# Sorted rows: eight places in the first mixture part, and adding gathers for the second batch's results

## What is computed

```
x = x + 0.5 * moe(layernorm(x))
x = x + attention(layernorm(x))
x = x + 0.5 * moe(layernorm(x))

moe(x):    for each row pick the expert with the largest logit (8 experts), rw = sigmoid(top logit)
           g = (rw * x) @ w_gate[e].T ; u = (rw * x) @ w_up[e].T ; y = (u * silu(g)) @ w_down[e].T
attention: 8 heads of 64, keys and values from a latent of 64, softmax over 1024 keys, output projection
```

## Time and profile before

| | us |
|---|---|
| median of 3 runs | 1085.79 |
| the three runs | 1084.59, 1085.79, 1086.81 |
| profiled execution, own time | 1084.6 |
| its span, first to last instruction | 1082.8 |
| busy in the span: PE, DVE, POOL, ACT | 968.5, 704.0, 693.9, 483.8 |
| mean granted TensorE clock (1 is full) | 0.957 |

### The profile page before, as it was taken

One profiled execution on the slowest core, in us unless ns is written; L12 is line 12 of the kernel. 1 busy time (PEld: TensorE's weight loads), 2 busy tenths in 40 slices (PEclk: granted clock), 3 DMA queues, 4 the chain that ended last, 5 costly groups with the idle time before them and its releaser, 6 DMA issues.

```text
span 1082.8 us, 14843 instructions
## 1 busy us (share of the span) xinstructions
PE 968.5 (89%) x5084; PEld 519.7 (48%) x5084; DVE 704.0 (65%) x1197; ACT 483.8 (45%) x794; POOL 693.9 (64%) x400
## 2 busy tenths in 40 slices
PE   5799866999899899999999999999999998954995
PEld 3488633444344544444455444444544443443784
DVE  5765587477777746777765676776666676743563
ACT  4673322544444264444433444444244446331562
POOL 1345530899899366777854767786278788836554
PEclk9799966999999999999999999999999999967998
DMA  9365521212202100000010000001000300053321
GB/s 326 126 196 152 149 69 59 65 39 51 68 12 74 69 2 1 1 1 1 1 69 1 1 0 2 1 1 44 26 1 1 118 1 1 33 161 105 118 87 42
DMA packets 41688, 61.52 MB, mean 57 GB/s; under 512 B 7114, under 2 KB 35278, under 8 KB 40592
## 3 DMA queue, kind: packets, MB, share of 16 engines
q1 hardware_dynamic: 23616, 31.26, 8.6%
q0 software_dynamic: 9024, 18.69, 6.5%
q10 hardware_dynamic: 8976, 10.63, 2.8%
HBM read 28.28 MB, written 26.64 MB: 51 GB/s over the span
## 4 chain that ended last, share of the span: by engine, by line
PE 67%; DVE 17%; POOL 5%; ACT 3%; issue 3%; another core or an unknown queue 3%; DMA 1%; POOLq 0%; ACTq 0%; DVEq 0%
PE ps_o L1377 16%; PE ps L1364 11%; PE ps L1171 8%; DVE maxes L1177 7%; PE ps L835 7%; DVE rows_store L1749 5%; PE ps_x L1151 5%; POOL arena_b L1853 4%; PE ps L1530 3%; PE ps_x L1399 2%; PE ps_o L853 2%; PE ps L819 2%; PE ps_x L694 1%; PE ps_x L1243 1%
## 5 line engine op out<-in xcount | busy, mean ns | idle before, releaser
L1177 DVE TENSOR_REDUCE maxes<-ps 128x2 f32<-128x1024 f32 x256 | 310.8, 1217 | 195.4 <-PE ps L1171 194.8
L1853 POOL TENSOR_TENSOR arena_b<-arena_b 128x1024 f32<-128x1024 f32 x112 | 272.3, 2437 | 173.3 <-PE ps_o L1377 137.9
L1853 POOL TENSOR_TENSOR arena_b<-arena_b,hot_store 128x1024 f32<-128x1024 f32 x108 | 263.6, 2441 | 60.7 <-PE ps_o L1377 28.6
L1364 PE MATMUL ps<-q_split,keys_now 64*128 64x512 f32 x1536 | 205.5, 392 | 0.0
L1618 ACT ACTIVATE arena_b<-ps 128x1024 f32<-128x1024 f32 x144 | 143.2, 1022 | 101.5 <-PE ps L1364 101.4
L1364 PEld LDWEIGHTS ps<-q_split,keys_now 64*128 64x128 f32 x1536 | 145.2, 185 | 33.1 <-issue 4.1
L1377 PE MATMUL ps_o<-arena_b,latent_now 128*64 128x512 f32 x576 | 147.2, 613 | 1.3 <-ACT arena_b L1618 1.3
L1618 ACT ACTIVATE hot_store<-ps 128x1024 f32<-128x1024 f32 x112 | 111.9, 1021 | 57.4 <-PE ps L1364 57.4
L1377 PE MATMUL ps_o<-hot_store,latent_now 128*64 128x512 f32 x448 | 115.2, 610 | 2.6 <-ACT hot_store L1618 2.5
L1749 DVE RECIPROCAL rows_store<-rows_store 128x256 f32<-128x256 f32 (+1 forms) x72 | 112.6, 1565 | 6.5 <-ACT rows_store L1629 6.5
L835 PE MATMUL ps<-arena_a,arena_b 128*128 x368 | 100.9, 398 | 0.9 <-DVE arena_b L985 0.5
(11 more groups left out here) (294 smaller groups left out, 1155.6 us busy)
## 6 DMA issues: line engine op xcount, KB each, us to landing
sorted_y<-arena_b ACTq DMA_DIRECT2D x46, 128.0 KB
x_res<-sorted_x SPq DMA_DIRECT2D x32, 130.0 KB
x_res<-x_in SPq DMA_DIRECT2D x4, 1024.0 KB, 13.6
scaled_x<-rows_store SPq DMA_DIRECT2D x16, 256.0 KB, 2.1
keys_now<-keys_next SPq DMA_DIRECT2D x4, 1024.0 KB, 4.6
sorted_x<-blank SPq DMA_DIRECT2D x2, 1560.0 KB
sorted_x<-blank SPq DMA_DIRECT2D x2, 1430.0 KB
arena_a<-w_gu SPq DMA_DIRECT2D x1, 2048.0 KB, 15.6
```

The costliest lines, as they stand in the source:

```text
L1177: nc.vector.tensor_reduce(maxes[:, 2 * m:2 * m + 2], bank[:, :, :], AX_X, ALU.max) \
L1364: last = nc.tensor.matmul(ps_s[n % 2][:, a, :], keys_now[h, key, k], query[h, p, q], start=False, stop=(kt >= KT - STRIDE and query is q_h ...
L1853: nc.gpsimd.tensor_tensor(t, t, prob(k, kt).rearrange("p a n -> p (a n)"), ALU.add) \
```

## The change

The ring of sorted rows in f1 gets eight places instead of four; rows_back moves to the start of arena_b, over the raw weights, and leaves its room to the larger ring. POOL waits for the folds before the first gather back. DVE's adding of tiles 0 to 7 starts at step 39 instead of 43 and is spread over eleven steps (tiles at steps 40, 41, 43, 44, 45, 47, 48, 49). Tiles 8 to 15 are no longer gathered into rows_back and added by DVE: POOL joins them with eight adding gathers, which wait for nothing but their place in POOL's order. DVE waits for each four of them after one half of the keys, takes their statistics there, and makes the variance after the second half.

```diff
+IN_RING = {"f1": 8, "f2": RING}
-BACK_AT = SLOT_TILES - 3
+BACK_AT = SLOT_TILES - 7
...
-        rows_back = take(RING, D)
-        rows_in = take(RING, D)
+        rows_back = arena_b[:, 0:RING * D].rearrange("p (b n) -> p b n", b=RING)
+        rows_in = take(IN_RING["f1"], D)
...
-                h, k = t // AHEAD_TILES, t % RING
+                h, k = t // AHEAD_TILES, t % IN_RING["f1"]
...
-                if t >= RING:
-                    pool.wait_ge(sem("in_turned"), t - RING + 1)
+                if t >= IN_RING["f1"]:
+                    pool.wait_ge(sem("in_turned"), t - IN_RING["f1"] + 1)
...
+            pool.wait_ge(sem("folded"), 2 * PAIRS)
             for t in range(JOINED):
                 k = t % RING
-                if t >= RING:
+                if RING <= t < QT:
                     pool.wait_ge(sem("ffn_added"), t - RING + 1)
...
+                if t >= QT:
+                    pool.indirect_dma_start(x_tile(t), None, sorted_y[0][:, :],
+                                            bass.IndirectOffsetOnAxis(ap=slots[:, t:t + 1], axis=0),
+                                            compute_op=ALU.add).then_inc(sem(f"second{(t - QT) // GROUP}"), 16)
+                    continue
...
             for i in range(ROW_PAIRS):
                 dve_norm_rows(dve, 0, i)
-                gathered(QT + i)
-            for t in range(QT + ROW_PAIRS, JOINED):
-                gathered(t)
-            dve_variance(dve, "att", QT, JOINED)
             for j in range(2):
                 dve_keys(dve, 0, j, banks[4 + j])
+                dve.wait_ge(sem(f"second{j}"), 16 * GROUP)
+                for t in range(QT + j * GROUP, QT + (j + 1) * GROUP):
+                    tile_stats(t, "att")
+            dve_variance(dve, "att", QT, JOINED)
```

More of the change, by code:

```diff
@@ L219, in row_out @@
                 return sem(f"row_out{k}"), 16 * turn
-            name, uses = (("in{}_f1", len(range(k % RING, SLOT_TILES, RING))), ("gathered{}", JOINED // RING),
+            name, uses = (("in{}_f1", len(range(k % RING, SLOT_TILES, IN_RING["f1"]))), ("gathered{}", QT // RING),
                           ("joined{}", GROUP))[k // RING - 3]
@@ L811, in turn @@
                 if tag == "f1":
-                    pe.wait_ge(sem(f"in{k % RING}_f1"),
-                               16 * (t // RING + 1) if isinstance(t, int) else (t - k % RING) * 4 + 16)
+                    pe.wait_ge(sem(f"in{t % IN_RING['f1']}_f1"), 16 * (t // IN_RING["f1"] + 1))
                 else:
@@ L819, in turn @@
                     last = nc.tensor.transpose(banks[k % 2][:, c * P:(c + 1) * P],
-                                               source[:, k % RING, c * P:(c + 1) * P], ident[:, :])
+                                               source[:, t % IN_RING[tag], c * P:(c + 1) * P], ident[:, :])
                 last.then_inc(sem("in_turned"), 1)
```

## The result

The changed kernel takes 1091.2 us (median of 10 runs, 1088.96 to 1097.8) against 1084.95 for the kernel before beside it (1083.54 to 1088.24). The ratio is 1.0057, 95% interval 1.004 to 1.0074. The prediction said 1086.0, no measurable change, with a range that ends at 1089.2. It is slower, outside the range. The profiled execution took 1090.11 us with a span of 1088.3, 5.5 us more than before. One execution of experiment 10 (1204.59 us) and one of experiment 12 (5121.62 us) lay far above the others, and the ratios leave them out.

What follows compares the result with a forecast made beforehand. Bounds: PE in f1, then a chain hopping between engines, then DVE's maxima. Terms -1.5 - 0.9 + 2.6 = +0.2 us on the profiled 1084.6 gave 1084.8, median 1086.0; range 1082.6 to 1089.2.

Steps and rivals of the forecast that it cites:

- Eight places: Sorted gathers of f1: POOL four tiles further ahead, gathers back about 7 us earlier, DVE's adds earlier; gain 1.5 us.
- I take nothing: DVE's two early adds in f1 fit beside PE's matmuls and cost 0; 0.4 us if PE had no cover.
- the same five DMAs near 121 us: Last sorted gather and four gathers back, 1.26 us apart: same pace beside the same stores, only 7 us earlier.
- The last sorted gather at 113.4: End of f1: POOL issues its last sorted gather near 113.4 instead of 120.37 us, needing tile 37 turned, not 41.
- The stall near 126 us, taken as 0: Late f1, PE's steps 3.79 us apart, 2.1 lost: unchanged; bounds -2.1 if it goes, +2.1 if it comes twice.
- The rival that had it go: The stall near 126 us in f1 disappears, saving 2.1 us: 1083.9 us; chance 0.25.
- Slower, by a second stall: Rival: the eight adding gathers, at 134 to 149 us, bring another stall: 1088.6 or 1090 us; chance 0.16.
- nothing happened: Argument against a second stall: adding gathers are 1.86 us apart, and gathers 1.62 us apart had caused none.
- The square root, gain 1.5: Batch 0's variance after f1: square root right behind ACT's table load, at 138.4 instead of 139.95; gain 1.5 us.
- The turns, gain 0.9: Four PE turns before the latents, without DVE's adds between: last starts 3.3 us after the first, not 4.2; gain 0.9.
- The statistics behind the keys, loss 2.6: Eight statistics and variance moved into DVE's chain before the maxima: loss 0.35 + 2.25 us; bounds 0 and 3.7.
- Load on the DMA engines: Near 126 us: transfers from different engines share 16 DMA engines, so moving gathers among the same stores wins nothing.

Runs made afterwards that it cites:

- experiment 10: experiment 9 with four of the moved statistics ahead of the first keys, four with the variance between the key halves; 1083.81 us, ratio 1.0001.
- experiment 12: experiment 4 with two gaps of 1.4 us in the first 16 scatters of f2, behind the fifth and tenth; 1079.22 us, ratio 0.9962.
- experiment 1: The changed kernel with four places and DVE's adds from step 43 again, the rest of the change kept; 1085.47 us, ratio 1.002.
- experiment 2: The kernel before with eight places, rows back over raw weights, adds from step 39, second batch joined as before; 1087.19 us, ratio 1.0036.
- experiment 7: The changed kernel with a shorter POOL pause (128x256 memset) behind all 46 sorted gathers and the first four gathers back; 1085.01 us, ratio 0.9984.
- experiment 4: The kernel before with a POOL memset and wait behind its last sorted gather and first four gathers back; 1080.29 us, ratio 0.9969.
- experiment 3: The changed kernel with pauses behind its first twelve sorted gathers, eight at the half switch, the last, and four gathers back; 1088.13 us, ratio 1.0036.
- experiment 11: experiment 9 with the eight moved statistics reading 16 of 256 columns, part of the layer norm left out; 1080.19 us, ratio 0.997.
- experiment 9: experiment 1 with the pauses of experiment 4; 1082.96 us, ratio 0.9996 against the kernel before.
- experiment 6: The kernel before with 24 plain loads of 128 rows by SP into an unused buffer, POOL's gathers unchanged; 1084.76 us, ratio 0.9991.
- experiment 5: The kernel before with three more POOL gathers behind sorted gather 27 into unused places, still four ring places; 1091.13 us, ratio 1.0049.
- experiment 13: The changed kernel with eight gaps of 1.4 us in its sorted gathers, and pauses behind the last and four gathers back; 1087.22 us, ratio 1.0017.
- experiment 8: experiment 4 with the same pause also behind each of the 32 scatters at the start of f2; 1088.79 us, ratio 1.0025.

## Why the prediction was wrong

**Eight places: the step that failed.** "I take nothing" looked at DVE's two early adds and at the end of f1. It took the ring's lead as something that costs nothing to gain. But POOL can only gain a lead by issuing faster than PE uses, and that is the dense run. The prediction knew its effect from the earlier trace rows, and counted the same five DMAs near 121 us; it did not ask where four more places make new runs. There are two, twelve gathers at the start and five at the half switch. They cost 4.9 and 2.0 us in the trace; net of what the ring gains, experiments 1 and 2 both put it at about 4 us. The rows that would have told are in the trace of before, where POOL waits for PE's transposes among the first twelve gathers:

```profile
54.12 0.95 POOL L765 DMA_INDIRECT arena_b<-scaled_x,token_of  x1 [2.67 <-PE ps L819]
```
With eight places that wait goes, and the run becomes longer.

**The last sorted gather at 113.4.** It came at 120.68. The delay of 7.3 us took what the ring was to give. In experiment 7, without stalls, it was 115.98.

**The stall near 126 us, taken as 0.** It stayed, and PE's two steps there are 3.81 us apart, as before. The rival that had it go was wrong for this kernel; experiment 4 shows that 3 us lie in it, by the medians. The upper end of the range, 1089.2, is 3.2 us above the forecast, though a second stall of this size was priced at 2.55 (1088.6); the measured time lies above both. For the row itself the prediction had the right suspect.

**Slower, by a second stall.** The side and the mechanism of this rival were right, its place was not. The adding gathers are 1.84 to 1.89 us apart, landed 3.7 to 4.2 us after issue (3.6 predicted), and nothing stalled beside them. In the prediction's own words against it, at 1.62 us "nothing happened": this held for them. In experiments 3 and 7 no engine waited at such a pace for work that PE had finished, but DVE's small instructions were stretched.

**The square root, gain 1.5.** Right: 1.53 us, right behind its table load. In experiment 2 1.54.

**The turns, gain 0.9.** 1.28, with part of the turns at the higher clock. That the latents would start 2.4 us nearer to the last down product became 2.8.

**The statistics behind the keys, loss 2.6.** Right in size, for the first part by luck: the second keys start 0.29 us later against the first (0.35 predicted), but not because four statistics filled an idle 0.95 us. The latents came so fast that nothing was idle there, and the four took their full 1.3 us of the chain. From there to the first maximum it takes 6.39 us instead of 4.21, 2.18 more (2.25 predicted). What was missing is behind it: PE's wait of 3.26 us and the slower queries, 1.1 us more (experiment 11 takes both back together). And the latents at 3.70 us instead of 6.61 gave 1.8 us back in this execution; in experiment 1 they took 5.87 us. By single traces the part behind f1 therefore lies between -1.0 and +2.3 us, by the medians of experiments 1 and 9, which have four places and so no gain at the square root, between +2.2 and +2.9.

**Load on the DMA engines.** The sentences that draw on the Trainium skill (DMA: Bandwidth & Descriptors, Issuing engines are not separate DMA queues) had transfers of different engines share and interleave. The gathers back did run with the same stores and nothing was won on them, but experiment 6 had the engines at 0.88 with no stall: shared engines did not cause this one.

The Trainium skill (DMA: Bandwidth & Descriptors, SWDGE vs HWDGE vs iDMA) also says that for transfers started by POOL, software computes the descriptors and writes them into rings in SBUF, while hardware makes those of SP and ACT. Experiments 5 and 6 fit this, POOL's transfers held others up and SP's did not, but they also differ in form, indirect against plain. Which part of the issue does it, no run here shows.

**Left open.** What in a dense run withholds a signal: the traces show that POOL issues, that PE has finished, and that the waiting engines go on about 1 us (experiment 13) to 2.3 us (the first stall) after POOL's last issue of the run, or within it. That it is PE's signal, and not something in each waiting engine, is argued from ACT and POOL going on together, at 55.27 and 55.55. Loading of their code is not it in the first stall: in the kernel after, the DMA queues for instructions move no packet from 45 to 60 us. How many in a row it takes is not settled either: the kernel before issues six 1.26 us apart from 37.37 to 43.87 us, and experiment 12 five and six scatters, with no such wait, and experiment 13 has waits at four. Open too is when DVE's instructions are stretched. In experiment 3 two of them end with the memset or the gather of POOL under which they ran, but under a gather of the kernel before (54.12 to 55.07) the same ones take 0.23 us at most. The trace of after itself does not show the stretched DVE instructions as clearly as experiments 7 and 13, so their share in its loss is not known.

## What to carry to other kernels

A deeper prefetch ring lets the issuing engine run ahead, and the time in which it gains its lead is a burst: look for that burst at the start, and after each point where the ring runs empty, and ask what it does to everybody else. When several engines wait for an engine that has finished, and one issues indirect DMAs without a gap, try a pause there before anything bigger; it took 3 us off this kernel. Put it only where the burst is, since pauses may cost too: with one behind each of the first twelve gathers PE was 3 us later by the seventh tile, without such a stall (experiment 3). Pace only transfers that nobody awaits, and price work that is moved behind a bound engine with the clock of the engine that it leaves idle.

## What the runs showed of the hardware

- In runs of POOL's indirect DMAs 1.26 us apart, ACT, DVE and POOL waited up to 4.8 us for work that PE had finished, and DVE up to 8.3 with scatters. Where they were 1.56 to 1.89 us apart (the adding gathers, and parts of experiments 3, 4, 7 and 8), no such wait was seen.
- 24 plain loads of 128 rows within 23 us, at a DMA share of 0.88, held up nothing.
- In experiments 3, 7 and 13, with POOL issuing or filling memory most of the time, small DVE instructions took longer: those of 128x8 up to 0.64 us instead of 0.17.
- Latents of the same eight matmuls took 3.70 us in four traces (after, experiments 9, 11 and 13), where the granted clock was 1.00 over them, 5.33 in experiment 10 (0.69), 5.87 in experiment 1 (0.63) and 6.61 in the kernel before (0.57). Single traces differ by 3 us for that alone.
